# Wavelet attention with a mixture of experts: a new order at three places, and fourteen gathers ahead of the first scatter

## The reference

```python
low = x                                   # normed input
for _ in range(2):                        # two wavelet levels, 4 taps each, stride 2
    l = dwconv(low, h_filter)[:, ::2]
    h = dwconv(low, g_filter)[:, ::2]
    highs.append(h); low = l
low = linear_attention(low, 16)           # q = k = elu(h) + 1, num / den
for h, L in zip(reversed(highs), reversed(lens)):
    low = dwconv(repeat(low, 2), h_synth) + dwconv(repeat(h, 2), g_synth)
x1 = x0 + layer_norm(x + low, gamma, beta)

scores = sigmoid(h @ gate_w.T)            # h: normed x1; 16 experts
topk_score, topk_ids = top_k(scores.T, 256)    # each expert picks 256 of the 2048 tokens
eo = silu(xin @ gw + gb) * (xin @ up_w + up_b)  # F = 512, per expert, xin = h[topk_ids]
eo = eo @ down_w + down_b
out = zeros.at[topk_ids].add(eo * topk_score)
out = x1 + out + shared(h)                # shared: silu(h @ g) * (h @ u) @ d, 256 hidden
```

## Time and profile before

| | |
|---|---|
| Median of 3 runs | 214.35 us (214.26 to 214.61) |
| The profiled execution, and its span | 215.54 us, 213.6 us |
| TensorE, VectorE busy | 182.9 us (86%), 129.6 us (61%) |
| ScalarE, GpSimd busy | 89.5 us (42%), 121.6 us (57%) |
| Chain that ended last, by engine | TensorE 44%, VectorE 17%, transfers 14%, GpSimd 9%, issue 8% |
| Mean granted TensorE clock | 0.959 |

### The profile page before, as it was taken

One profiled execution on the slowest core, in us unless ns is written; L12 is line 12 of the kernel. 1 busy time (PEld: TensorE's weight loads), 2 busy tenths in 40 slices (PEclk: granted clock), 3 DMA queues, 4 the chain that ended last, 5 costly groups with the idle time before them and its releaser, 6 DMA issues.

```text
span 213.6 us, 3635 instructions
## 1 busy us (share of the span) xinstructions
PE 182.9 (86%) x1210; PEld 158.7 (74%) x1210; DVE 129.6 (61%) x431; ACT 89.5 (42%) x238; POOL 121.6 (57%) x175
## 2 busy tenths in 40 slices
PE   7789889999979899789899999999998899989000
PEld 7758769999836676559799999999897799978000
DVE  4879999999678888798444444444424444444000
ACT  0676603267586765110034444444434344434100
POOL 7610006546044467504776788878788777775550
PEclk9999999999999999996999999999999999999655
DMA  5699999500300550101422333323333233332221
GB/s 149 209 418 425 414 413 420 228 0 3 110 3 0 150 208 2 49 3 52 115 64 49 38 44 43 48 43 51 38 41 44 37 37 42 38 38 28 25 25 12
DMA packets 11618, 22.21 MB, mean 104 GB/s; under 512 B 1488, under 2 KB 8784, under 8 KB 11472
## 3 DMA queue, kind: packets, MB, share of 16 engines
q1 hardware_dynamic: 5968, 17.52, 21.6%
q0 software_dynamic: 5632, 4.46, 15.3%
HBM read 17.65 MB, written 4.33 MB: 103 GB/s over the span
## 4 chain that ended last, share of the span: by engine, by line
PE 44%; DVE 17%; DMA 14%; POOL 9%; issue 8%; ACT 3%; POOLq 1%; SPq 1%; DVEq 0%
DMA out_dram<-area,rows 11%; PE bank L1341 7%; PE bank L1342 7%; PE bank L1326 6%; PE bank L1080 6%; POOL out_dram L486 6%; PE bank L1035 4%; DVE junk L888 4%; DMA x_tok<-in_x_dram 2%; POOL sh_hid L460 2%; PE bank L1233 2%; PE bank L1097 2%; PE bank L1183 2%; DMA hT<-h_rows,rows 1%; DVE area L739 1%
## 5 line engine op out<-in xcount | busy, mean ns | idle before, releaser
L486 POOL DMA_INDIRECT out_dram<-area,rows x32 | 50.6, 1582 | 17.5 <-DMA out_dram<-area,rows 9.4
L1020 DVE SCALAR_TENSOR_TENSOR area<-bank,consts,sgate 128x256 f32<-128x256 f32 x64 | 30.9, 483 | 40.5 <-ACT sgate L670 40.5
L670 ACT ACTIVATE sgate<-bank,consts 128x256 f32<-128x256 f32 x64 | 30.2, 472 | 59.5 <-PE bank L1342 59.5
L1326 PEld LDWEIGHTS bank<-wT,area 128*128 128x128 f32 x256 | 38.4, 191 | 3.6 <-DVE area L1020 0.4
L1341 PE MATMUL bank<-area,wT 128*128 128x256 f32 x128 | 38.5, 383 | 1.6 <-issue 1.4
L1326 PE MATMUL bank<-wT,area 128*128 128x128 f32 x256 | 38.8, 275 | 0.2 <-DVE area L1020 0.2
L474 POOL DMA_INDIRECT hT<-h_rows,rows x32 | 32.0, 1000 | 11.4 <-issue 8.8
L1342 PE MATMUL bank<-area,wT 128*128 128x256 f32 x128 | 38.1, 379 | 0.0
L1342 PEld LDWEIGHTS bank<-area,wT 128*128 128x128 f32 x128 | 24.3, 190 | 3.3
L1035 PE MATMUL bank<-ident 128*128 128x128 f32 x164 | 23.9, 306 | 1.6 <-POOL ident L381 1.6
L1035 PEld LDWEIGHTS bank<-ident 128*128 128x128 f32 x164 | 22.4, 219 | 2.2 <-POOL ident L381 1.6
(11 more groups left out here) (186 smaller groups left out, 252.3 us busy)
## 6 DMA issues: line engine op xcount, KB each, us to landing
wT<-in_weights_dram SPq DMA_DIRECT2D x16, 768.0 KB, 16.5
h_rows<-hrow SPq DMA_DIRECT2D x2, 576.0 KB, 3.3
x_tok<-in_x_dram SPq DMA_DIRECT2D x4, 256.0 KB, 3.9
x_tok<-in_down_b_dram SPq DMA_DIRECT2D x1, 1024.0 KB, 7.2
out_dram<-x SPq DMA_DIRECT2D x4, 256.0 KB, 2.7
hT<-h_rows,rows POOLq DMA_INDIRECT x32, 2.6
out_dram<-area,rows POOLq DMA_INDIRECT x32, 3.3
sh_wT<-in_shared_dram SPq DMA_DIRECT2D x1, 384.0 KB, 2.9
```

The costliest lines, as they stand in the source:

```text
L486: pool.indirect_dma_start(out=out_rows, in_=eo[:, e % 2, c, :], in_offset=None, out_offset=bass.IndirectOffsetOnAxis(ap=rows[:, g, c, k:k ...
L670: act.activation(sgate_e[:, q % SGB, :], up_bank(q)[:, CAP:2 * CAP], ACT.Silu, bias=biasT[:, 1, j, e:e + 1]).then_inc(s_sil, 1)
L1020: dve.scalar_tensor_tensor(hidden[:, e % 2, j, :], up_bank(q)[:, 0:CAP], biasT[:, 0, j, e:e + 1], sgate_e[:, q % SGB, :], ALU.add, ALU.mul ...
L1326: last = pe.matmul(bank[3 + e % 2][:, c * P:(c + 1) * P], hidden[:, e % 2, j, c * P:(c + 1) * P], wT[:, e, 2, j, :], start=(j == 0 and c = ...
```

## The change

`AHEAD` goes from 13 to 14 and the seventh entry of `BETWEEN` from 2 to 1, so the order of the chunks stays. On ScalarE the sigmoid of the gate scores and `keep_hT(0)` move behind the first `count_third`. On VectorE line 777 moves behind the masking, and `level1_even(2)` behind the attention products. `WARM_C` goes from 10 to 4.

```diff
-    AHEAD = 13
-    BETWEEN = (2, 2, 2, 2, 2, 2, 2, 1, 1, 1, 1, 1, 0, 0, 0, 0)
+    AHEAD = 14
+    BETWEEN = (2, 2, 2, 2, 2, 2, 1, 1, 1, 1, 1, 1, 0, 0, 0, 0)
...
                            ACT.Sigmoid).then_inc(s_score, 1)
-            act.activation(hrow[:, :, C:ROW].rearrange("p (k r) e -> p k r e", r=2),
-                           logits[:, :].rearrange("p (r e k) -> p k r e", r=2, e=E), ACT.Sigmoid).then_inc(s_hrow, 1)
-            keep_hT(0)
...
                 count_third(r)
+                if r == 0:
+                    act.activation(hrow[:, :, C:ROW].rearrange("p (k r) e -> p k r e", r=2),
+                                   logits[:, :].rearrange("p (r e k) -> p k r e", r=2, e=E), ACT.Sigmoid).then_inc(s_hrow, 1)
+                    keep_hT(0)
...
-            link(dve.tensor_scalar(r1_even, h2p[:, :, 0:N2], tap_sum(1, 0), None, ALU.mult))
             dve.wait_ge(s_masks, 1)
             dve.wait_ge(s_kv, 1)
...
                               same8[:, :].unsqueeze(1).to_broadcast([P, NB, P]), ALU.mult).then_inc(s_kvm, 1)
+            link(dve.tensor_scalar(r1_even, h2p[:, :, 0:N2], tap_sum(1, 0), None, ALU.mult))
             link(level1_even(1, r1_even))
-            link(level1_even(2, r1_even))
...
                                   ALU.mult).then_inc(s_attn, 1)
+            link(level1_even(2, r1_even))
             dve.wait_ge(s_attnT, 1)
...
-            WARM_I, WARM_E, WARM_S, WARM_L, WARM_C = 5, 3, 6, 3, 10
+            WARM_I, WARM_E, WARM_S, WARM_L, WARM_C = 5, 3, 6, 3, 4
```

## The result

The changed kernel took 214.01 us in the median of 20 executions (213.46 to 216.01), and the kernel before, run beside it, 215.18 us in the median of 20 (214.26 to 217.76). The ratio is 0.995, with a 95% interval of 0.9926 to 0.9974: faster by 1.17 us between the medians, against a forecast of 1.66, and above the upper end of the range, 213.6.

What follows compares the result with a forecast made beforehand. It took the bound as TensorE with VectorE to about 147 us, then GpSimd scatter issue alternating with transfer. Attention 0, search −1.14 and GpSimd −0.52 sum to −1.66: 214.35 to 212.7 us, range 212.1 to 213.6.

Steps and rivals of the forecast that it cites:

- Search: Start of the threshold search: fewer warm-ups and ScalarE's earlier count bring the first decision and later rounds 1.14 us forward.
- the hT copy: ScalarE in search round two: copy done at 56.97 us, first shared matmul pair waits for it, no gain lost.
- the two rivals here: Search, both slower: clock falls to 1.2 GHz, 214.9 us, chance 0.06; ScalarE reloads tables, 216.0 us, chance 0.03.
- Attention: Linear attention on VectorE: masking's earlier half microsecond is spent on the third tap before the copy; 0, bounds ±0.2 us.
- the forecast wait of 0.2: VectorE in the attention: a new wait of 0.2 us opens ahead of the denominators.
- GpSimd: Queue of gathers and scatters: first scatter 0.42 us later, shortened seventh gap gives 0.94 back; net −0.52 us.
- its first half: GpSimd's first scatter: fourteenth gather costs 1.24 us, 0.81 falls into the wait for expert 0, so 0.42 later.
- The second half of the step: GpSimd's seventh gap: losing a gather shrinks it from 6.42 to 5.48 us, the transfer's round trip; 0.94 us gained.
- the first rival: First scatter held by GpSimd all along: extra gather costs 1.24 us, net +0.30, time 213.5 us; chance 0.16.
- The base: Whole kernel: the profiled execution's 1.19 us excess over the 214.35 us timed median was assumed to stay.

Runs made afterwards that it cites:

- order_only: The kernel before with only the new order on ScalarE, ten warm-ups kept; ratio 1.0025, median 215.74 us.
- hold_before: The kernel before, thirteen gathers ahead, with four added warm-ups around the first table product and transpose to hold the clock; ratio 1.0018, median 216.13 us.
- attn_only: The kernel before with only the two moved VectorE operations of the attention; ratio 1.0018, median 216.39 us.
- hold_pool: The kernel before with four clock-holding warm-ups added, fourteen gathers ahead and one less in the seventh gap; ratio to the kernel before 0.9969, median 214.91 us.
- pool_only: The kernel before with only the fourteenth gather ahead and one gather less in the seventh gap; ratio 1.002, median 216.23 us.
- ahead13: The changed kernel with thirteen gathers ahead and two in the seventh gap again; ratio to the kernel before 0.9919, median 213.42 us.
- after_again: The changed kernel run once more, nothing altered, beside the kernel before; ratio 0.9908, median 213.45 us over ten executions.
- the held pair: The kernel before with four clock-holding warm-ups added, with thirteen and then fourteen gathers ahead; medians 216.13 and 214.91 us.
- the last comparison: The last four follow-up kernels, the changed kernel's repeat among them, run beside the kernel before, whose median there was 215.64 us.
- warm_only: The kernel before with four warm-ups instead of ten ahead of the first count, ScalarE's order as before; ratio 1.0019, median 215.58 us.

## Why the prediction was right, and where it was wrong

**Search: right.** −1.14 was forecast, −1.13 came, and −1.12 with the edit alone. The reason held too: VectorE's count releases the first decision, either half of the edit alone does less (0.51 and 0), and the hT copy (done at 57.08, against a forecast of 56.97) holds TensorE for 0.62 us; behind it the second decision waits 0.17 us for TensorE, but the third, which hangs on the table load, still comes 1.13 earlier. Of the two rivals here, the clock stayed at 1.00 in the profile's rounds, and no table was loaded. The Trainium skill, "ScalarE: Activation LUTs", "What ACT_TABLE_LOAD costs", prices a switch at 2.66 us, about 1283 ns of load and about 1380 ns of drain. This trace agrees with the load (1.28 us at 57.66) and shows no drain: the next activation starts at 58.95.

**Attention: right within its bounds.** 0 ± 0.2 was forecast, 0.11 gained, with the forecast wait of 0.2 at the forecast place. The experiment confirms the interval, not a gain in the time.

**GpSimd: wrong, in its first half.** The failed step is "That is **0.42 later**: of the 1.24 us that a gather costs, 0.81 falls into the wait." It read the 1.11 us of idle time in one execution as slack that every execution has. That execution had a fallen clock at 97 us and a mean of 0.959. Of 102 executions of the kernel before that ran beside the experiments, 11 had a mean of 0.960 or less; the mean is only a hint, since `order_only`'s profile has 0.960 with a fall at 12 to 18 us and a clock of 1.00 from 88 to 112. When the clock holds, thirteen gathers already hold the first scatter (115.30 in `hold_before`, 115.49 in `attn_only`), so the fourteenth costs its whole turn: 1.26 or 1.27 in three pairs (`hold_before` and `hold_pool`, `attn_only` and `pool_only`, `ahead13` and `after_again`). The second half of the step, the gap that shrinks to the round trip, was right in the changed kernel: it gives back 0.94 (5.49 after gaps of 6.43). In `hold_pool` and `pool_only` it gives back less, 0.79 and 0.74 (gaps of 5.64 and 5.69). Net it is +0.29 (`ahead13` against the change) to +0.50 (the held pair), not −0.52. This is the first rival, which had +0.30 and a chance of 0.16. Its reason stood in the prediction, which said that the fall "can turn out either way"; it was given too small a chance on the strength of one trace and three times.

**The sum, redone:** −1.13 − 0.11 + 0.30 = −0.94, or −0.74 with the held pair's +0.50. The cleanest check is the last comparison. There the kernel before falls into two groups by eye, 15 executions of 214.03 to 214.83 (median 214.38) and 18 from 215.44 up. The changed kernel's ten are all in one, with a median of 213.45: −0.93. In the first comparison the split is less clear; the lower 11 of the kernel before (to 215.33, median 214.61) and the lower 15 of the changed kernel (to 214.37, median 213.89) give −0.72. Over all executions the medians are 1.17 apart there (215.18 to 214.01) and 2.19 in the last comparison (215.64 to 213.45). What goes beyond the sum is a smaller share of long executions: 5 of 20 and none of ten for the changed kernel, against 18 of 33 for the kernel before in the last comparison. No term of the prediction has it, and which edit does it, if any, stays open. The first rival's own time, 213.5, is near that 213.45.

**The base: wrong too.** "I assume that the difference stays" took 214.35, a median of three, for the kernel's time. The median of 20 is 215.18, because many executions end one to three microseconds later than the lowest. The three happened to lie low. With the right sum, 214.35 − 0.94 = 213.4 would have been the time of the undisturbed executions alone; the 214.01 is a median over a mixture, of which 15 of 20 lie at 213.46 to 214.37 and five at 214.94 to 216.01. The right base alone would have given 215.18 − 1.66 = 213.5; both together give 215.18 − 0.94 = 214.2, which is near 214.01. So 213.6, the range's upper end, fell short by the wrong sign of one term and by the low base together.

**Why the profile agreed anyway.** It compared an execution with a fallen clock to one whose clock held. Relative to the first gather, the first scatter moved from 116.22 − 98.55 = 17.67 us to 115.79 − 97.66 = 18.13, by +0.46, which looks like the forecast +0.42. In the held pair, where only the queue differs, the same step is +1.27. The 0.81 that the forecast hid in a wait was that wait of a fallen clock, which the second execution would not have had with thirteen gathers either. The sums agree; the reason does not.

## What to carry to other kernels

A wait in one profile is slack only if it is there in most executions: look at the granted clock ahead of it, and at the mean clock and span of other executions, before you let an edit fall into it. Where a queue and a compute chain meet, find the crossing by moving the queue by one step each way; here it lay between twelve and thirteen gathers, and the lowest spans of thirteen and fourteen, run side by side, are 211.0 and 211.2, that of twelve, in another comparison, 211.8, because the gaps give back most of what the start costs. Two edits that release the same instruction are worth less apart and are to be costed together, as the search's two halves were.

## What was not expected of the hardware

Single executions of one kernel spread over one to four microseconds (before: 214.03 to 218.13 in the last comparison). Two sources were seen in profiles.

**The clock fell early in some.** In `ahead13` it fell in the first wavelet level, and four matmuls that take 1.88 us in the profile of the change took 3.58. The rows are from TensorE's timeline, first of the changed kernel and then of `ahead13`, and from the windows of `ahead13`:

```profile
13.43 1.88 PE L1053 MATMUL bank<-area,diag 128*128 128x512 f32 x4
```

```profile
13.62 3.58 PE L1053 MATMUL bank<-area,diag 128*128 128x512 f32 x4
```

```profile
12.00:14.00 2.00, 1.33 (x9) 1.05 (x9) 1.91 (x6) 1.98 (x5) 0.00 (x0) 0.90 1.01 415
14.00:16.00 2.00, 2.00 (x3) 0.67 (x2) 1.91 (x3) 1.10 (x3) 0.00 (x0) 0.50 1.01 416
16.00:18.00 2.00, 2.00 (x8) 0.96 (x7) 0.00 (x0) 0.33 (x1) 0.00 (x0) 0.74 1.03 427
```

The changed kernel's row was at a clock of 1.00; its program is the same up to there. `warm_only` and `order_only` showed the same fall in 12 to 18 us, and all three were late by about 2 us from there on.

**A scatter's completion arrived late in others**, always behind the tenth or eleventh. GpSimd's and VectorE's timelines of `attn_only`, and its window:

```profile
173.34 1.56 POOL L486 DMA_INDIRECT out_dram<-area,rows  x1 [0.30 <-issue]
...
178.91 1.58 POOL L486 DMA_INDIRECT out_dram<-area,rows  x1 [2.69 <-DMA out_dram<-area,rows]
```

```profile
178.74 0.42 DVE L1011 TENSOR_TENSOR area<-bank,x_tok 128x256 f32<-128x256 f32 x1 [2.77 <-DMA out_dram<-area,rows]
```

```profile
176.00:178.00 2.00, 2.00 (x16) 1.87 (x14) 0.00 (x0) 0.47 (x1) 0.23 (x1) 1.00 0.28 54
178.00:180.00 2.00, 0.24 (x4) 0.08 (x2) 1.15 (x3) 0.80 (x3) 1.09 (x1) 1.00 0.00 0
```

Both engines that wait for that scatter were released together. From its start at 171.46 to the next scatter's it took 7.45 us, where the other such gaps take about 5.4, and no transfer was in progress from 178 us to the release at 178.7. Five profiles showed it (6.8 to 7.45 us). Why it happens at that scatter stays open, and so does whether it is what made nine executions of `hold_before` long and only three of `hold_pool`: no run here changed the transfers of a scatter to find out.
